# Grouped-query attention on one Trainium2 core: next rows transposed in the middle of a projection, and four parts moved in the engines' lists

## The reference, cut to what matters

```python
x = x + attn(layernorm(x))                  # x: 64 sequences x 64 rows x 256
# attn: 16 query heads, 4 key/value heads, head size 128
q, k, v = split(h @ w_qkv.T)
q = layernorm(q, qn_g, qn_b); k = layernorm(k, kn_g, kn_b)
q = q * cos + rotate_half(q) * sin;  k = k * cos + rotate_half(k) * sin
w = softmax(causal(q @ k.T / sqrt(128)))
attn = (w @ v) @ w_o.T
```

## Time and profile before

| what | value |
|---|---|
| three timed runs | 3211.05, 3217.69, 3225.68 us; median 3217.69 |
| the profiled execution | 3207.37 us, its span 3205.5 us |
| the attention stage with the change | from about 40 to 922 us of the span |
| granted TensorE clock, mean | 0.943 |
| busy over the whole span | PE 83%, DVE 63%, ACT 49%, POOL 43% |

### The profile page before, as it was taken

The page is one execution under the profiler, slowest core; times in us unless marked ns, Lnnn a source line. Parts: engine busy times, 40 slices in busy tenths (PEclk is TensorE's granted clock), DMA queues, the critical chain, the costliest instruction groups (busy, mean ns, idle before and its releaser), DMA issues. The chain is left out here.

```text
span 3205.5 us, 85997 instructions
## 1 busy us (share of the span) xinstructions
PE 2644.7 (83%) x33006; PEld 1936.5 (60%) x33006; DVE 2030.2 (63%) x3706; ACT 1581.7 (49%) x2950; POOL 1372.7 (43%) x1490
## 2 busy tenths in 40 slices
PE   3888888888858888867677779999999999997565
PEld 2677777777732222224466667888788888886333
DVE  6888888888858888848577743434343434334776
ACT  3555555555527777731334313443434444443566
POOL 4888888888822333224222212222222212221665
PEclk9999999999969999979799989999999999999667
DMA  3000000000013333300100020000000000000000
GB/s 120 2 0 0 0 0 0 0 0 0 0 49 89 89 90 90 92 13 0 31 24 25 26 69 6 7 6 7 6 7 6 7 6 7 5 33 1 13 16 23
DMA packets 94784, 77.50 MB, mean 24 GB/s; under 512 B 17520, under 2 KB 88560, under 8 KB 93424
## 3 DMA queue, kind: packets, MB, share of 16 engines
q1 hardware_dynamic: 94576, 74.35, 7.6%
HBM read 55.97 MB, written 17.04 MB: 23 GB/s over the span
## 5 line engine op out<-in xcount | busy, mean ns | idle before, releaser
L1394 DVE TENSOR_REDUCE x_mx<-x_ps 128x2 f16<-128x512 f32 x512 | 330.8, 682 | 47.0 <-PE x_ps L1458 44.5
L1363 ACT ACTIVATE x_e<-x_ps 128x512 f32<-128x512 f32 x512 | 291.9, 596 | 46.2 <-PE x_ps L1462 30.2
L361 POOL TENSOR_TENSOR x1s<-x1s,x1mx 128x1024 f32<-128x1024 f32 x32 | 60.9, 1902 | 542.3 <-DVE x1mx L357 542.3
L1722 ACT ACTIVATE x_q<-x_ps,x_q_bias,x_q_scale 128x128 f32<-128x128 f32 x512 | 186.1, 467 | 162.0 <-PE x_ps L105 161.9
L1458 PE MATMUL x_ps<-x_k,x_q 32*128 32x256 f16 x1024 | 194.7, 281 | 82.4 <-ACT x_e L1363 53.1
L431 ACT CAST x1oh<-x_ps 128x1024 f16<-128x1024 f32 x64 | 64.7, 1012 | 328.9 <-PE x_ps L423 328.9
L103 PE MATMUL a_ps<-ln_xha,a_wq 128*128 128x128 f16 x1024 | 181.0, 222 | 51.3 <-ACT a0v L678 43.8
L1458 PEld LDWEIGHTS x_ps<-x_k,x_q 32*128 32x128 f16 x1024 | 58.7, 92 | 261.6 <-DVE x_mx L1394 126.2
L627 POOL TENSOR_TENSOR a_w<-a_qsw,a_tab 128x512 f32<-128x512 f32 x128 | 176.8, 1381 | 58.1 <-ACT a_qsw L688 56.7
L1462 PE MATMUL x_ps<-x_q,x_k 32*128 32x256 f16 x1024 | 196.5, 283 | 1.7 <-ACT x_e L1363 1.4
L280 DVE TENSOR_TENSOR ln_xlx<-x_ps,ln_xhx 128x256 f16<-128x256 f32 x32 | 13.6, 424 | 289.0 <-ACT x_xt L1714 289.0
(11 more groups left out here) (365 smaller groups left out, 9120.4 us busy)
## 6 DMA issues: line engine op xcount, KB each, us to landing
x_q<-x_q_rows SPq DMA_DIRECT2D x32, 256.0 KB, 2.8
x_k<-x_k_rows SPq DMA_DIRECT2D x32, 256.0 KB, 3.1
a_stage<-in_x_w SPq DMA_DIRECT2D x32, 256.0 KB, 2.6
x_vt<-in_ctx_v SPq DMA_DIRECT2D x32, 144.0 KB, 2.3
stage<-in_x_wt SPq DMA_DIRECT2D x4, 1028.0 KB, 6.4
x_all<-in_x SPq DMA_DIRECT2D x8, 512.0 KB, 9.9
x_cf<-in_ctx SPq DMA_DIRECT2D x32, 128.0 KB, 2.1
x_q_rows<-x_xhl SPq DMA_DIRECT2D x32, 128.0 KB, 1.7
```

What stands on the lines that cost most here:

```text
L1363: act.activation(e[:, u % ES].rearrange("p c n -> p (c n)"), s2_ps(u), ACT.Exp, scale=XT ** -0.5).then_inc(e_ready, 1)
L1394: dve.reduce_max(mx[:, p % 2, c:c + 2], s1_ps(u), AX).then_inc(mx_ready, 1)
L1722: last = act.activation(q[:, i, :], ps[:, bank(4 + g), h * P:(h + 1) * P], ACT.Identity, scale=q_scale[:, i:i + 1], bias=q_bias[:, i:i + 1])
```

## The change

Five edits in `attention_gqa` and its helpers:

1. The layer norm's transposes go to bank 2, the bank of query group 0, instead of bank 0. `next_rows` then waits for the first `rotate_query` of the tile instead of the third.
2. On TensorE `next_rows` stands in the middle of the second projection half, between its fourth and its fifth head, instead of behind it.
3. On ScalarE the value copy and `high(t-1, 1)` stand ahead of the exponential instead of behind it.
4. On ScalarE `ln.high(t+2)` stands ahead of `square(t+1, 3)` instead of behind it.
5. On VectorE `low(t-1, 1)` and `ln.normalise(t+2)` stand ahead of `denominator(t)` instead of behind it, and `ln.low(t+2)` stands ahead of the second `add_swapped`.

No instruction is added or taken away.

```diff
-    def project(self, pe, t, r, last_tile=False):
+    def project(self, pe, t, r, last_tile=False, first=0, end=8):
         pe.wait_ge(self.ol_ready, 2 * t + 1 + r)
         ...
-        for j in range(8):
+        for j in range(first, end):
         ...
-        if r:
+        if r and end == 8:
             last.then_inc(self.y_ready, 1)
...
-        ln = LayerNorm(m, ctx, sem, "a0", ps[:, 0, :])
+        ln = LayerNorm(m, ctx, sem, "a0", ps[:, 2, :])
...                                                     # ScalarE
-                at_.exponential(act, t)
-                if has_next:
                     value(t + 1, 1 - p)
                 if before:
                     at_.high(act, t - 1, 1, not has_next)
+                at_.exponential(act, t)
                 if has_next:
                     square(t + 1, 2)
-                    square(t + 1, 3)
                 if further(t):
                     ln.high(act, t + 2, p, q_ready, 4)
+                if has_next:
+                    square(t + 1, 3)
...                                                     # VectorE
-                at_.denominator(dve, ch, t)
                 if before:
                     at_.low(dve, t - 1, 1, not has_next)
                 if further(t):
                     ln.normalise(dve, t + 2, p)
+                at_.denominator(dve, ch, t)
                 if has_next:
                     rotate_query(t + 1, 2)
+                if further(t):
+                    ln.low(dve, t + 2, p)
+                if has_next:
                     add_swapped(t + 1, 1)
                     rotate_query(t + 1, 3)
                 if before:
                     at_.add(dve, t - 1)
-                if further(t):
-                    ln.low(dve, t + 2, p)
...                                                     # TensorE
-                pe.wait_ge(u_ready, 4 * (t - 1) + 3)
+                pe.wait_ge(u_ready, 4 * (t - 1) + 1)
                 ln.transpose(pe, t, p)
...
-                    at_.project(pe, t - 1, 1)
+                    at_.project(pe, t - 1, 1, end=4)
                 if further(t):
                     next_rows(t + 2, p)
+                if before:
+                    at_.project(pe, t - 1, 1, first=4)
```

## The result

| what | before | after |
|---|---|---|
| timed runs, median (lowest to highest) | 3217.08 us (3211.05 to 3225.68, 4 runs) | 3267.57 us (3260.12 to 3275.31, 4 runs) |
| ratio after / before, 95% interval | | 1.0155 (1.0120 to 1.0191) |
| span of the profiled execution | 3205.5 us | 3269.8 us |
| end of the attention stage (start of the next layer norm's epsilon) | 924.4 us | 985.9 us |
| period, from the second to the 31st L796 | 26.40 us | 28.59 us |

The change makes the kernel 1.6% slower, 50.5 us, where 3186 us was forecast and 3176 to 3224 given as the range. The interval lies clear of 1. Of the 64.3 us more in the span, 61.5 are there when the attention stage ends: 63.6 in 29 periods, 2.8 less before the second tile, 2.9 more in the last of the pipelined steps, 2.2 less in the closing.

What follows compares the result with a forecast made beforehand. The attention stage was taken as a loop of waits, limited after the change by GpSimd's loop: 25.54 against 26.49 us. 29 x 0.95 = 27.6, less 0.4, plus 4.1 gave 31.3: median 3217.7 to 3186, range 3176 to 3224.

Steps and rivals of the forecast that it cites:

- `query_sums` waiting for GpSimd: TensorE, ready for `query_sums` at 622.6, would wait some 1.9 us a tile for GpSimd's last `squares_low`.
- the later `squares_low` at 1.15: GpSimd's `squares_low` of groups 2 and 3 would take 1.15 us and not 1.60.
- the `add_swapped` held instead: VectorE's third and fourth `add_swapped` would start 0.07 us behind GpSimd's `squares_low` and not hold it.
- The terms of the loop: `query_sums` to `query_sums` through GpSimd: 9.79, 4.66, 3.53 and 7.56 us, together 25.54 against 26.49.
- the third term: From GpSimd's second product (group 1) to its L381: 3.53 us, or 4.50 if L262 loses the port.
- the closing step: After the last tile, the probabilities' transposes would no longer stand behind the projection: 4.1 us won.
- By these L262 wins: it takes 0.41: VectorE's L262 starts 0.07 us before GpSimd's `squares_low` of group 1, gets the shared port and takes 0.41 us.
- the first rival: L262 loses the port to GpSimd's `squares_low`: loop 26.51 us, nothing won in it, 3215 us in total; chance 0.34.
- the sum of the waits a tile falls: Argument against the clock falling: TensorE's waits per tile shrink, and the clock was 1.00 with over three us of them.
- The price of a fall: A lower clock between `query_sums` and GpSimd's first product would add 2.5 us to a tile.
- The bounds, 1.0 to 4.7: Least and most us a lower clock could add a tile between `query_sums` and GpSimd's first product.
- the clock rival: TensorE's longer wait before `query_sums` lowers the clock: slower, 3259 us with all tiles at 1.2 GHz; chance 0.06.

Runs made afterwards that it cites:

- the quiet kernel of experiment 3: Changed kernel plus a 128x1 GpSimd addition before group 1's `squares_low` and 16 unused TensorE matmuls before `query_sums`; 3157.73 us, ratio 0.9834 to the kernel before.
- the kernel with 12 matmuls: Changed kernel plus 12 unused 128x256 f16 TensorE matmuls in front of `query_sums`; 3193.93 us, ratio 0.9944 to the kernel before.
- the edit on ScalarE alone: Kernel before with only the value copy and `high` moved ahead of the exponential on ScalarE; 3245.89 us, ratio 1.0080 to the kernel before.
- Experiment 6: Changed kernel plus 4 unused TensorE matmuls in front of `query_sums`; 3219.22 us, ratio 1.0004 to the kernel before.
- the pause: Changed kernel plus one unused 128x1 GpSimd addition (0.18 us) between `swapped_part` and `squares_low` of group 1; 3227.52 us, ratio 1.0066 to the kernel before.
- the filler in the kernel before: Kernel before plus 12 unused 128x256 f16 TensorE matmuls in front of `query_sums`, no other edit; 3229.73 us, ratio 1.0065 to the kernel before.

## Why the prediction was wrong

**The steps that held.** The order on ScalarE, no wait for the value copy, `query_sums` waiting for GpSimd, the later `squares_low` at 1.15 and the `add_swapped` held instead are in the trace. TensorE still waits before the keys, 10.4 us in 19 tiles: less than the 35.3 of before, though I had written that any such wait would make the forecast wrong altogether. The terms of the loop were right to 0.1 us. In the full-clock tile after the change: Q to the first product 133.21 - 123.41 = 9.80 (9.79 predicted), to the second 4.67 (4.66), to L381 4.48 (4.50 for a lost port), to the next Q 7.55 (7.56). In the tiles of the kernel with pause and 16 matmuls the third term is 3.53 to 3.54 (3.53 predicted). In the closing step the transposes no longer stand behind the projection:

```profile
968.74 1.09 PE L391 MATMUL a_ps<-ident,a0e 128*128 128x128 f32 x8 [2.30 <-POOL a0e L381]
```

From the last L796 to the stage's end it is 33.5 us after the change and 31.9 in the quiet kernel of experiment 3, against 35.7: 2.2 and 3.8 won, 4.1 predicted.

**First failed step: "By these L262 wins: it takes 0.41".** In 16 of 29 tiles, the one at full clock among them, it took 1.34 and gave the first rival. I had a reason among the rival's: L262 held its data back for 0.26 us, L758 only 0.14. I set the bare order of starts above it. A lead of 0.02 to 0.05 loses; one of 0.19 wins, and so does 0.33. The trace of the kernel before had a tile with a lead of 0.20 that I left out of the prediction; L262 wins there, and L381 takes 1.95 instead of 1.90:

```profile
86.45 0.40 DVE L262 TENSOR_SCALAR ln_xna<-x_all,ln_mva,ln_rstda 128x256 f32<-128x256 f32 x1
```

```profile
86.65 1.95 POOL L381 TENSOR_TENSOR a0e<-a0e,a0rden 128x1024 f32<-128x1024 f32 x1
```

Where between 0.05 and 0.19 the limit lies, and whether it is the time at which L262 asks for its data, no run shows. The Trainium skill ("SBUF — State Buffer", Who interferes with whom) says that issue order decides who blocks; the start in the trace isn't that order here, since the one that starts 0.04 earlier was blocked. In a tile at full clock this step costs 1.0 us (26.50 against 25.45), and so, with the clock held, the whole gain of 27.6 us: the kernel with 12 matmuls, where 22 of 29 tiles lose the port, shows 26.3 to 26.5. In the kernel as it ran it cost 0.9 to 1.0 us in 16 tiles (29.4 to 29.5 against 28.5 with a fall of 6.8 us, 27.8 against 27.0 with one of 3.4), some 15 us.

**Second failed step: the clock, "Against it: the sum of the waits a tile falls".** I gave it 0.06, and it decided the sign. The sum did fall, from 3.7 us a tile (35.3, 28.6 and 13.6 us of TensorE's waits in 21 tiles) to 2.9 (33.2, 12.1 and 10.4 in 19), and the clock fell all the same. The third of the waits before, not shown so far:

```profile
PE a_ps L103 <- DVE a0ol L437: 13.6, 21, 0.7
```

In the edit on ScalarE alone two waits that were harmless apart are one of 2.39 and cost 29 falls. In the changed kernel the wait before `query_sums` is 2.1 behind a tile in which L262 lost, with two of 0.6 and 0.66 in the 7 us before it. I had the length nearly right (1.9) and compared it with the 1.7 that stand before the keys today, as if only length counted. Experiment 6 shows that it doesn't: in front of `query_sums` 1.45 us, and even 0.8, is enough.

**A size.** The price of a fall was 2.5 us a tile. With the pause, a tile with a fall of 6.8 us takes 28.4 to 28.6, one of 3.4 us 26.9 to 27.0, one without 25.35 to 25.53: 3.0 and 1.4. From Q to GpSimd's first product it is 12.7 instead of 9.8. The bounds, 1.0 to 4.7, held it.

**How they add.** The two rivals were priced as if only one could come. Both came, and each acts on the other: a lost port makes the wait longer (2.1 against 1.8), and the falls rise from 21 to 27; and all 13 tiles in which L262 won have the clock at 0.50 for a part of them. Of the 3.1 us a tile between the quiet loop of 25.45 and the 28.59, about 0.5 is the port (16 tiles of 29) and about 2.5 the clock (an estimate from the prices above: 21 falls of 6.8 us at 3.0, 6 of 3.4 at 1.4). With the median at 3268 the kernel is slower than even the clock rival's 3259, whose sum had every tile at 1.2 GHz but the port won.

**Still open.** What exactly lets the clock fall: 10 falls behind waits of 0.8 before `query_sums`, none with 1.7 before the keys. That waiting TensorE at this place brings the falls on is shown by filling it; why this place, and not the length or the busy share alone, is not. Whether the edits on VectorE alone would help with the clock held wasn't run apart.

## What to carry to other kernels

When a change moves TensorE's waits to another place, price the clock first, even if their sum falls: one long wait can cost what two short ones didn't, and in front of many small matmuls a short one is enough. The price here was 3.0 or 1.4 us a fall. Where two engines come to the shared port within 0.1 us of each other, take neither as the winner until a run shows it, and move one of them: 0.18 us of delay gave 1 us back in a tile at full clock. Look at every tile, too: here the race was lost in 16 and won in 13. And compare kernels by the stage that was edited, since the total can move by 20 us elsewhere.

## What the runs showed of the hardware

- TensorE at clock 1.00 fell to 0.50 after stretches in which it still worked 3.80 of 6.50 us, in another kernel 5.72 of 6.50, and came back by itself while it worked. In the kernel before a stretch with 4.17 of 6.50 had no fall. Matmuls put into the wait cut the falls from 27 to 10 (12 of them) or, with the pause, from 21 to 6 (12) and 0 (16). The same matmuls elsewhere left 29.
- L262 with a `tensor_tensor` of GpSimd (`squares_low`) 0.02 to 0.05 us behind it takes 1.34 us, with one 0.19 behind it 0.40, and then costs GpSimd 0.08 (1.23 against 1.15). An addition of 128x1 only 0.05 behind it didn't hold it.
- TensorE stood 13 times for up to 1.6 us, in a stage that no edit touches (the second layer's cross-attention), for nothing that the profile shows; in the eight kernels whose TensorE program is longer by the filler these waits were gone, and with the filler in the kernel before the stage was 22 us shorter.
